# Second normalisation of the state in L3_attn, by GpSimd instead of VectorE and one slot sooner

## What is computed

```python
x = _layernorm(x + _L3_attn_ref(x, L3_attn_Wq, L3_attn_Wk, L3_attn_Wv, L3_attn_Wo), axis=-1)
x = _layernorm(x + _L3_xattn_ref(ctx_1024, x, mask_BxS2_bk0, L3_xattn_g1, ...), axis=-1)

def _L3_xattn_ref(x, latents, mask, g1, b1, g2, b2, Wq, Wkv, Wout):
    xn = layer_norm(x, g1, b1)
    ln_lat = layer_norm(latents, g2, b2)      # latents is the state
    q = ln_lat @ Wq
    kv = jnp.concatenate([xn, ln_lat], axis=1) @ Wkv
    ...
```

## Time and profile before

| | |
|---|---|
| runs of the kernel before | 1721.30, 1721.54, 1727.79 us (median 1721.54) |
| profiled execution, its own device time | 1723.16 us |
| its span (first to last instruction) | 1721.4 us |
| mean granted TensorE clock | 0.976 of full speed |
| busy: TensorE, VectorE, ScalarE, GpSimd | 93%, 81%, 72%, 44% of the span |
| L3_attn, sequences 0 to 11 | from about 1235 to 1339 us of the span |

### The profile page before, as it was taken

How to read it: one execution, slowest core, us unless ns; L and a number is a source line. 1 busy time by engine, 2 the same in 40 slices (tenths; PEclk the granted TensorE clock), 3 DMA queues, 4 the chain that set the end, 5 groups by cost and what they waited for, 6 DMA issues and landing times. The chain is left out here.

```text
span 1721.4 us, 42296 instructions
## 1 busy us (share of the span) xinstructions
PE 1607.3 (93%) x14878; PEld 1210.8 (70%) x14925; DVE 1396.5 (81%) x4091; ACT 1236.2 (72%) x4825; POOL 764.9 (44%) x976
## 2 busy tenths in 40 slices
PE   8999999999989998779999999788888999999998
PEld 7886568999855565336668888556555677888877
DVE  6777887778889999898867878688899877777775
ACT  4557997666599999349984444386799777788775
POOL 2235882000166787467751111021677544445455
PEclk9999999999987899899999999889999999999999
DMA  9001000000000000000000000205000000111100
GB/s 301 1 2 40 2 2 2 2 2 2 2 2 2 2 2 2 1 1 2 2 2 2 2 2 2 94 22 223 2 2 2 1 2 14 50 50 50 62 27 26
DMA packets 16002, 43.28 MB, mean 25 GB/s; under 512 B 5681, under 2 KB 9009, under 8 KB 13873
## 3 DMA queue, kind: packets, MB, share of 16 engines
q1 hardware_dynamic: 15792, 40.58, 6.7%
HBM read 29.04 MB, written 11.53 MB: 24 GB/s over the span
## 5 line engine op out<-in xcount | busy, mean ns | idle before, releaser
L1869 POOL TENSOR_TENSOR a_probs<-a_probs,a_rinv 128x512 f32<-128x512 f32 (+1 forms) x288 | 272.4, 948 | 160.6 <-DVE a_rinv L1707 156.3
L1473 ACT ACTIVATE a_probs<-bank,a_negmax 128x128 f32<-128x128 f32 x896 | 327.4, 444 | 18.5 <-DVE a_negmax L1672 14.4
L1869 POOL TENSOR_TENSOR c_probs<-c_probs,c_rinv 128x512 f32<-128x512 f32 x192 | 200.2, 1043 | 187.3 <-DVE c_rinv L1707 184.1
L1473 ACT ACTIVATION_READ_ACCUMULATOR a_probs<-bank,a_negmax 128x1 f32 x896 | 244.9, 285 | 0.0
L1917 POOL TENSOR_TENSOR a_rstd<-a_ve,neg_half 128x1 f32<-128x1 f32 x128 | 70.4, 550 | 298.3 <-DVE a_ve L1760 297.2
L1264 PEld LDWEIGHTS bank<-const,a_probs 128*128 128x128 f32 x1024 | 115.7, 144 | 113.6 <-issue 96.8
L1264 PE MATMUL bank<-const,a_probs 128*128 128x128 f32 x1024 | 174.2, 289 | 2.4 <-POOL a_probs L1869 1.4
L1676 DVE TENSOR_REDUCE a_negmax<-bank 128x4 f32<-128x512 f32 x192 | 130.1, 679 | 16.2 <-PE bank L1235 16.0
L1246 PE MATMUL bank<-state_t,w_L_ffn 128*128 128x128 f32 x1024 | 135.9, 276 | 0.0
L1714 DVE COPY a_probs_t<-bank 128x512 f32<-128x512 f32 (+1 forms) x192 | 118.4, 617 | 14.7 <-PE bank L1264 14.4
L1508 ACT ACTIVATE c_probs_t<-bank 128x512 f32<-128x512 f32 x176 | 105.4, 599 | 33.3 <-PE bank L1264 32.3
(11 more groups left out here) (292 smaller groups left out, 4317.2 us busy)
## 6 DMA issues: line engine op xcount, KB each, us to landing
space<-kept_halves SPq DMA_DIRECT2D x20, 512.0 KB, 4.4
kept_halves<-stage SPq DMA_DIRECT2D x6, 1024.0 KB, 4.2
w_L_ffn<-in_L_ffn SPq DMA_DIRECT2D x1, 3184.0 KB, 21.6
w_L_xattn<-in_L_xattn SPq DMA_DIRECT2D x1, 2050.0 KB, 8.6
kept_halves<-xq SPq DMA_DIRECT2D x2, 1024.0 KB, 4.3
kept_halves<-xqt SPq DMA_DIRECT2D x2, 1024.0 KB, 4.7
w_L_xattn<-in_L_xattn SPq DMA_DIRECT2D x1, 1536.0 KB, 8.2
ctx_t<-in_ctxT SPq DMA_DIRECT2D x1, 1024.0 KB, 12.6
```

The source lines that it names most:

```text
L1473: op = act.activation(p, bank_of("scores", n)[:, j * width:(j + 1) * width], ACT.Exp, scale=-1.0 if plan.masked_by_dve(s) else 1.0, bias=n ...
L1869: pool.tensor_tensor(p, p, along(rinv[:, n % PB, 0:heads], wide(kind) // heads), ALU.mult).then_inc(sems["norm_done"], 1)
```

## The change

For L3_attn alone the second normalisation is issued by GpSimd, directly behind the power L1920 of the same slot, and its slot is 5 instead of 6 behind the step's last unit. It waits there for the same semaphore as before and raises the same one. VectorE no longer issues it for these 16 steps. For the 16 steps of L3_xattn, whose successor L3_ffn also has gain and bias, it stays on VectorE.

```diff
-    "normalise_again": {"all": 6, "mqa": 5, "h8p": 7, "moe": 8, "h64m": 7, "ffn": 4},
+    "normalise_again": {"all": 6, "mqa": 5, "h8p": 7, "moe": 8, "h64m": 7, "ffn": 4, "h8r": 5},
@@ VectorE
-                            if what == "normalise_again":
+                            if what == "normalise_again" and plan.next_kind(s) != "h64m":
                                 normalise_again(s)
@@ GpSimd
+                            if what == "normalise_again" and plan.next_kind(s) == "h64m":
+                                pool.wait_ge(sems["rstd2_ready"], 1 + sum(plan.affine_next(t) for t in range(s)))
+                                pool.tensor_scalar(LH[:, b % R_RING, :], X[:, b, :], mv2[:, b, 0:1], rstd2[:, b:b + 1], ALU.subtract, ALU.mult).then_inc(sems["norm2_ready"], 1)
                             if what == "normalise" and plan.affine_next(s):
                                 pool.wait_ge(sems["stat2_ready"], 1 + sum(plan.affine_next(t) for t in range(s)))
                                 pool.tensor_tensor(rstd2[:, b:b + 1], ve2[:, b:b + 1], neg_half[:, 0:1], ALU.pow).then_inc(sems["rstd2_ready"], 1)
```

## The result

| | before | with the change |
|---|---|---|
| device time, median of 20 runs each | 1724.03 us | 1720.35 us |
| ratio, 95% interval | | 0.9976 (0.9966 to 0.9986) |
| gain | | 4.1 us (2.4 to 5.9) |
| predicted | | 1712.2 us, a gain of 9.3 |

The kernel is 0.24% faster, 4.1 us where 9.3 were forecast, and its time lies outside the prediction's 1709.8 to 1717.0. Some of the miss in absolute time is the base: the three runs shown before had a median of 1721.54, twenty have 1724.03. The gain is what the rest of this text is about.

A forecast was written before the change was run, and what follows sets the result against it. It took L3_attn's loop of waits through L1775, 8.65 us a period, as the bound. The first turn's 0.60 plus 11 x 0.79 gave 9.3 us off 1721.54, so 1712.2 us, range 1709.8 to 1717.0.

The forecast's parts named there:

- What bounds the kernel now: In L3_attn a loop of waits through L1775 sets the 8.65 us period; some 0.85 of L1775's 1.18 is a stall.
- Removed from VectorE: L1775 leaves VectorE sixteen times; in twelve, VectorE's own work falls from 8.65 to 7.55 us a period, the last four nothing.
- Added to GpSimd: One TENSOR_SCALAR of 128x128 float32 behind the second power, sixteen times, at 0.30 us, bounds 0.30 to 0.455.
- The loop afterwards, what else binds: In L3_attn the loop falls to 7.83 us, ScalarE's own 7.86 is largest, so the period falls by 0.79.
- the floors: Each engine's own work per L3_attn period: TensorE 7.82, ScalarE 7.86, VectorE 7.55, GpSimd 6.64 us; no period can be shorter.
- Behind the added wait: GpSimd's first L1869 of a period starts 0.38 us later, costed at nothing; placing the operation behind it would be later.
- B: Rival: GpSimd needs twice VectorE's time for the operation, 0.67 us; loop 8.20, gain 5.4 us, 1716.1 us; chance 0.13.
- C: Rival: the stall moves to VectorE's L1765 or another instruction, 0.34 us more; gain 5.9 us, 1715.7 us; chance 0.10.
- D: Rival: waits between the full engines hold the period near 8.3; gain at most 3.9 us, 1718 us; chance 0.11.
- E: Rival: GpSimd's operation makes the turn later than now, from 1.12 us on; at 2.4 us, 1736.9 us; chance 0.04.

The follow-up runs named there:

- e1: The changed kernel with constants 0 and 1 for the mean and the power in GpSimd's second normalisation; 1716.86 us against 1722.46 for the kernel before.
- e6: The changed kernel with GpSimd's second normalisation as multiply and add, mean unscaled and of wrong sign; 1715.46 us against 1723.33 for the kernel before.
- e3: The kernel before, with GpSimd waiting for VectorE's second normalisation before its first multiplication of probabilities behind the second power; 1711.06 us against 1722.46.
- e5: The changed kernel with GpSimd's operation in its old slot, behind the first multiplication of probabilities; 1733.16 us against 1722.46 for the kernel before.
- e4: The kernel before, with the second normalisation kept on VectorE but one slot sooner (5); 1715.94 us against 1722.46.
- the second trial: The changed kernel with trial operations on GpSimd at the program's start, comparing arithmetic pairs, scalars and widths; ran once, 1730.39 us, total not read.

## Why the prediction was wrong

**What bounds the kernel now:** right. The loop over L1775, the turn, L1585 and L1770 sets the period. With the measured length of the operation it gives 8.33, 8.18 and 7.98 for the change, e1 and e6, and the traces show 8.35, 8.18 and 8.01. The stall behind GpSimd's L1869 is real, as e3 shows. What I did not see is a second hold of this kind in the same loop. The rotary sum L1617 starts while a GpSimd multiplication still runs, and takes 0.65; where none runs, it takes 0.42. Timelines of VectorE and GpSimd before, in the first sequence and in a later one:

```profile
1234.91 0.42 DVE L1617 TENSOR_TENSOR c_qk<-c_qk,c_rt 128x256 f32<-128x256 f32 x1
```

```profile
1277.29 1.04 POOL L1869 TENSOR_TENSOR c_probs<-c_probs,c_rinv 128x512 f32<-128x512 f32 x1 [0.37 <-DVE c_rinv L1707]
1277.95 0.65 DVE L1617 TENSOR_TENSOR c_qk<-c_qk,c_rt 128x256 f32<-128x256 f32 x1
```

It is 0.65 in every later period before and with the change, and 0.42 again in two periods of e5 (the ones of 10.7), where no multiplication is beside it. So 0.23 of the 8.35 left is this. No run takes it away, and what that would give is not shown.

**Removed from VectorE:** the operation is gone from there, and VectorE waits for TensorE instead. Its own work was put too high, 7.55 for 7.19, which didn't matter for the change and made the expectation of e4 wrong.

**Added to GpSimd: here it failed.** The step was "one TENSOR_SCALAR of 128x128 float32 with two scalars per partition ... I take 0.30, as it is the nearest row, and 0.30 to 0.455 as bounds". It takes 0.80, outside its own bounds. The two rows used, L1894 and L563, have the same operation name as the new one, and the rows don't show more. In the code L1894 multiplies and adds and L563 adds and multiplies; both are quick pairs. The change subtracts and multiplies. Of the 0.50 missed, 0.35 is the pair (e6) and the rest the two scalars per partition (0.15: 0.45 against 0.30 in the second trial, 0.80 against 0.65 in e1). The conclusion that scalars "add nothing visible" came from subtracting two rows that differed in type, width and arithmetic at once.

**The loop afterwards, what else binds:** the loop was right in every term but this one. With 0.80 it exceeds TensorE's 7.82 and so decides by itself; the floors, over which ScalarE was to be next, never came into play. TensorE's floor held in e3, ScalarE's would not have.

**Behind the added wait:** right. GpSimd's first L1869 starts 0.77 behind the operation's start instead of 0.38, and TensorE shows no wait for it; the slot matters as said (e5).

**The rivals:** B was the nearest, and for about its reason: the operation is long. It had 0.67 and 5.4 us; with 0.80 the same working gives 0.3 + 11 x 0.32 = 3.8. The Trainium skill (GPSIMD Engine Reference, section "Engine selection") has GpSimd about twice as slow as VectorE for two-input elementwise work and puts one-input operations at roughly line rate. Here the one-input operation took 2.3 times VectorE's 0.345, so with this pair the exception doesn't hold; with the quick pair it is 1.3 times. C did not happen: L1765 is at 0.334 in the middle of the stage, as before. D did not either. The point of E, 1.12 us, was not reached.

**The numbers:** B with 0.13 was too unlikely. The bounds for an operation without a row of its own were drawn from whichever rows were there, and the upper one was a two-input operation. Three runs were also too few for an absolute time to be put within 0.2%: base and result vary by more than that, and the gain alone would have been the better target.

## What to carry to other kernels

When an operation is priced by a row of another, look up what that other computes: same operation name, shape and type cost 0.45 or 0.80 us on GpSimd, by the arithmetic alone, and writing x - m as x + (-m) doubled what this change gains in L3_attn. Where VectorE is held up behind a GpSimd instruction, one wait that lets GpSimd start a little later can be worth more than the move to another engine (11.0 us here against 4.1), if GpSimd has the time. And a row without idle time can still hide a wait of some 0.1 us, so compare the distance of two starts with the same pair elsewhere before calling an engine's busy time its work.

## What the runs showed of the hardware

- TENSOR_SCALAR on GpSimd, 128 columns of float32: 0.30 us for multiply and add with constants, 0.65 for subtract and multiply with constants, 0.45 and 0.80 with two scalars per partition. A single multiplication (0.54 with a constant, 0.60 with a scalar per partition) is longer than a multiplication and an addition together.
- The slope is 0.9 ns a column for the quick pair and 3.3 for the slow one. At 16 columns they still take 0.35 and 0.43, so for narrow tiles the fixed part is nearly all.
- A 128x128 TENSOR_SCALAR on VectorE takes 0.32 to 0.35 alone and 1.18 when a 1.04 us GpSimd multiplication starts 0.05 behind it. That fits the lock of the Trainium skill (SBUF — State Buffer, section "SBUF: two separate sides"), which gives the pair to whichever starts first, but the one held up here was the instruction whose recorded start came first. When GpSimd's instruction starts 0.16 behind instead, VectorE's is not held: L1765 takes 0.34 at 1287.18, with L1844 beside it from 1287.34 on the earlier trace rows. So the recorded starts decide only when they are far enough apart; between 0.06 and 0.15 there is no row.
- A 128x256 TENSOR_TENSOR on VectorE (L1617) takes 0.42 alone and 0.65 when it starts 0.37 before the end of a GpSimd multiplication. No idle time in the trace shows this hold or the one above.
- TensorE's granted clock fell to 0.50 for some 3 us in two periods of e5, at a usual wait of 1.52 us a period, and never in the same stage of the change with its wait of 0.52.
